# A reduction over three weight matrices on ScalarE: its loads alternated between two borrowed buffers, and more of them issued per step

## The reference

```python
q = _rmsnorm(x @ wq.T + bq, gq).reshape(B, L, H, D)     # B=4, L=2048, H=16, D=128
k = _rmsnorm(x @ wk.T + bk, gk).reshape(B, L, H, D)
v = (x @ wv.T + bv).reshape(B, L, H, D)
...                                                     # scores on 16 shifts, softmax, mix of v
x = _layernorm(x + out @ wo.T + bo)

def _quantize(w):
    gamma = jnp.mean(jnp.abs(w))
    return jnp.clip(jnp.round(w / (gamma + 1e-8)), -1.0, 1.0)
def _bitlinear(x, w):
    return jnp.matmul(x, _quantize(w).T)
hidden = sigmoid(_bitlinear(x, w1)) * _bitlinear(x, w2)  # w1, w2: 5632 x 2048
x = _layernorm(x + _bitlinear(hidden, w3))               # w3: 2048 x 5632
```

## Time and profile before

| | us |
|---|---|
| runs, lower and higher | 8750.89, 9032.59 |
| median of the two | 8891.74 |
| profiled execution | 8730.72 |
| its span on the slowest core (core 4) | 8729.2 |
| spans of the eight cores | 8706.3 to 8729.2 |

### The profile page before, as it was taken

One profiled execution on the slowest core, in us unless ns is written; L12 is line 12 of the kernel. 1 busy time (PEld: TensorE's weight loads), 2 busy tenths in 40 slices (PEclk: granted clock), 3 DMA queues, 4 the chain that ended last, 5 costly groups with the idle time before them and its releaser, 6 DMA issues. The chain is left out here.

```text
span 8729.2 us, 69946 instructions; the slowest of 8 cores (8706.3 to 8729.2 us)
## 1 busy us (share of the span) xinstructions
PE 5297.4 (61%) x24300; PEld 2462.2 (28%) x24680; DVE 3486.7 (40%) x4731; ACT 678.8 (8%) x737; POOL 811.0 (9%) x468
## 2 busy tenths in 40 slices
PE   6878878688883017771200001882789778878883
PEld 3443433344331001111100001441334333333331
DVE  4222222422221014336768887227542441442424
ACT  0012222100222210000000000000000000000000
POOL 0000000000000003550074400000000001001000
PEclk7889988788896558995555555885889889889896
DMA  2222222221223331005643333002212113114114
GB/s 94 73 90 74 83 85 73 102 71 68 94 74 110 125 109 51 29 21 139 167 145 129 131 130 125 29 20 96 75 51 75 58 41 119 53 46 123 49 53 158
DMA packets 254343, 750.12 MB, mean 86 GB/s; under 512 B 119596, under 2 KB 119852, under 8 KB 193324
## 3 DMA queue, kind: packets, MB, share of 16 engines
q1 hardware_dynamic: 80820, 418.42, 14.6%
q10 hardware_dynamic: 163576, 295.74, 10.0%
q0 software_dynamic: 9600, 31.47, 1.2%
HBM read 630.20 MB, written 115.34 MB: 85 GB/s over the span
## 5 line engine op out<-in xcount | busy, mean ns | idle before, releaser
L71 ACT ACT_TABLE_LOAD x223 | 286.1, 1283 | 7595.2 <-DVE tiny L71 2411.6
L71 DVE SCALAR_TENSOR_TENSOR accb<-vwV,attn,accb 128x128 f32<-128x128 f32 x1200 | 654.9, 546 | 169.4 <-DMA vwV<-v_h 75.4
L71 POOL TENSOR_TENSOR prodb<-qe,knorm 128x1024 f32<-128x1024 f32 (+14 forms) x184 | 320.0, 1739 | 3596.7 <-DVE knorm L71 3568.0
L1070 PE MATMUL pt4a<-c_id,accb 128*128 128x128 f32 x64 | 17.4, 427 | 982.2 <-DVE accb L71 974.4
L1332 PE MATMUL pb<-x2T_lo,qwt 128*128 128x512 bf16 x1408 | 574.5, 408 | 11.5 <-issue 9.1
L1386 PE MATMUL pb<-qw3s,stash_hi 128*128 128x512 bf16 x1352 | 525.0, 388 | 75.8 <-DMA qw3s<-qw3t_h 54.0
L1387 PE MATMUL pb<-qw3s,stash_lo 128*128 128x512 bf16 x1408 | 546.4, 388 | 3.5 <-issue 0.7
L1303 PE MATMUL pb<-x2T_lo,qwt 128*128 128x512 bf16 x1408 | 534.4, 380 | 2.5 <-issue 0.2
L1331 PE MATMUL pb<-x2T_hi,qwt 128*128 128x512 bf16 x1321 | 535.4, 405 | 0.0
L1302 PE MATMUL pb<-x2T_hi,qwt 128*128 128x512 bf16 x1363 | 517.3, 380 | 0.0
L71 POOL DMA_DIRECT2D qw3s<-qw3t_h x176 | 96.1, 546 | 3414.1 <-PE pb L1387 1763.7
(11 more groups left out here) (215 smaller groups left out, 9392.5 us busy)
## 6 DMA issues: line engine op xcount, KB each, us to landing
gbuf<-w ACTq DMA_DIRECT2D x88, 1024.0 KB, 6.3
fw<-w SPq DMA_DIRECT2D x88, 1024.0 KB, 4.9
vwV<-v_h SPq DMA_DIRECT2D x74, 1024.0 KB, 4.8
vwG<-v_h ACTq DMA_DIRECT2D x47, 1024.0 KB, 5.5
gbuf<-w ACTq DMA_DIRECT2D x64, 704.0 KB, 4.1
fw<-w SPq DMA_DIRECT2D x64, 704.0 KB, 4.1
wfb<-wv SPq DMA_DIRECT2D x32, 1024.0 KB, 5.0
wfb<-wk SPq DMA_DIRECT2D x32, 1024.0 KB, 6.0
```

Of the source, the lines that this page charges most:

```text
L71: return fn(*a, **k)
```

## The change

- The tile `gbuf0` is gone. Jobs load into `xbuf[k % 2]`, where k counts the jobs.
- `_gS_block` issues the load of job k first and then waits for the load of job k-1 and computes on it. One job stays pending (`gpendS`) from one call of `emit_gamma` to the next; a call with `drain=True` also computes the last pending one.
- Two waits on ScalarE are new for each job: for `x_tp` up to the value it has behind `p1` of this half, and, from job 2 on, for the `Abs` of job k-2, which used the same buffer.
- `emit_gamma(4)` stands behind each strip in place of 3, and `emit_gamma(2)` behind each block in place of 1. The first half now does 4x4 + 32x2 = 80 jobs, the second 4x4 + 16x2 = 48, the last call the remaining 24, all of 704 KB.
- Ahead of `rs_build("q")` there is a call that only drains.

```diff
-    gbuf = [xsc.sb("gbuf0", [128, 2048])]
...
     g_emit = [0]
-
-    def emit_gamma(n):
+    gcntS = [0]; gpendS = [None]
+    gxtp = [0]
+
+    def _gS_block(e, jobs, drain):
+        gab = S("g_ab")
+        for (src, col, w) in jobs:
+            k = gcntS[0]; gcntS[0] += 1
+            e.wait_ge(S("x_tp").h, gxtp[0])
+            if k >= 2:
+                e.wait_ge(gab.h, k - 1)
+            sm = ring_issue("gld", k)
+            sm.inc(e.dma_start(out=xbuf[k % 2][:, 0:w], in_=src), 16)
+            ring_rec("gld", k, sm)
+            if gpendS[0] is not None:
+                pk, pcol, pw = gpendS[0]
+                ring_wait(e, "gld", pk)
+                gab.inc(e.activation(xbuf[pk % 2][:, 0:pw], xbuf[pk % 2][:, 0:pw],
+                                     ACT.Abs, accum_out=gacc[:, pcol:pcol + 1]), 1)
+            gpendS[0] = (k, col, w)
+        if drain and gpendS[0] is not None:
+            pk, pcol, pw = gpendS[0]; gpendS[0] = None
+            ring_wait(e, "gld", pk)
+            gab.inc(e.activation(xbuf[pk % 2][:, 0:pw], xbuf[pk % 2][:, 0:pw],
+                                 ACT.Abs, accum_out=gacc[:, pcol:pcol + 1]), 1)
+
+    def emit_gamma(n, drain=False):
         j0 = g_emit[0]; j1 = min(j0 + n, len(gamma_jobs)); g_emit[0] = j1
-        if j1 <= j0:
-            return
-        gab = S("g_ab")
-        def fa(e):
-            for ji in range(j0, j1):
-                src, col, w = gamma_jobs[ji]
-                sm = ring_issue("gld", ji)
-                sm.inc(e.dma_start(out=gbuf[0][:, 0:w], in_=src), 16)
-                ring_rec("gld", ji, sm)
-                ring_wait(e, "gld", ji)
-                gab.inc(e.activation(gbuf[0][:, 0:w], gbuf[0][:, 0:w], ACT.Abs,
-                                     accum_out=gacc[:, col:col + 1]), 1)
-        on("scalar", fa)
+        sjobs = [gamma_jobs[j] for j in range(j0, j1)]
+        if sjobs or drain:
+            on("scalar", lambda e, sjobs=sjobs, drain=drain: _gS_block(e, sjobs, drain))
...
-            emit_gamma(3)
+            emit_gamma(4)
...
-            emit_gamma(1)
+            emit_gamma(2)
...
     p1(0)
+    gxtp[0] = S("x_tp").n
     p2v(0)
     p2kq("k", 0)
     p2kq("q", 0)
+    emit_gamma(0, drain=True)
     rs_build("q")
     barrier(recycle=False)
     p1(1)
+    gxtp[0] = S("x_tp").n
     p2v(1)
     p2kq("k", 1)
-    emit_gamma(1000)
+    emit_gamma(1000, drain=True)
```

More of the change, by code:

```diff
@@ L328, in build_nc, with _gjob @@
     gamma_jobs = []
[L329 to L332, removed]
+    def _gjob(src_, w_):
+        gamma_jobs.append((src_, len(gamma_jobs), w_))
+    for nm in ("w1", "w2"):
+        for gt in range(44):
+            _gjob(ins[nm][gt * 128:(gt + 1) * 128, :], 2048)
     for dt_ in range(16):
         for qt in range(4):
-            gamma_jobs.append((ins["w3"][dt_ * 128:(dt_ + 1) * 128, qt * 1408:(qt + 1) * 1408],
-                               88 + dt_ * 4 + qt, 1408))
+            _gjob(ins["w3"][dt_ * 128:(dt_ + 1) * 128, qt * 1408:(qt + 1) * 1408], 1408)
```

## The result

| | before | after |
|---|---|---|
| timed runs: median (lowest to highest), us | 8930.62 (8724.12 to 9275.65), 10 runs | 8456.79 (8314.93 to 8787.2), 11 runs |
| profiled execution, us | 8730.72 | 8331.64 |
| its span on the slowest core, us | 8729.2 | 8330.1 |
| median span of cores 0 to 3, of cores 4 to 7, us | 8715.8, 8722.8 | 8310.4, 8317.5 |

The changed kernel takes 0.9525 of the time before, 95% interval 0.9499 to 0.9551. The forecast was 8331 us, by the terms 0.953 of the profiled execution before (8320.6 / 8730.7).

A forecast was written before the change was run, and what follows sets the result against it. Bound: the core waiting on ScalarE's serial load and `Abs` turns before the square root. Profiled 8730.7 - 412.1 + 2.0 = 8320.6 us, plus half of 20 us for timed runs: 8331 us, range 8295 to 8465.

The forecast's parts named there:

- The bound: First stage, 2732 to 3208 us: the core waits on serial load and `Abs` turns; TensorE's wait for the square root is 494.9 us.
- The tail's length: The 24 jobs left after the last block: last `Abs` ends at 2795.6 instead of 3207.7 us, saving 412.1 us.
- a job's turn: Time per job after the last block: 2.89 us, as two jobs share 5.78; bounds 2.1 and 5.78 us.
- The weighing of the two loads: Whether two loads in flight overlap, 2.89 us a job, or serialize whole, 4.1 us a job with 383 us saved.
- The trace's side: Two 1 MB loads in flight landed in 6.1 and 8.1 us, one alone in 4.9: only the transfers queue up.
- The end of the first half: Last jobs and draining call before the first half's square root: +2.0 us, 0 if the load is quick, up to +5.
- What was costed at nothing: Extra jobs in blocks and at strip turns, weight loads beside them, new waits and TensorE's clock: all taken as 0 us.
- the covers: Time hiding the added work: 16.8 us ScalarE idle per block, 15.0 us per `wfb` load, next store at 255.96 us.
- Rival 2: At the 8 strip turns `wfb` lands late, giving back 16 to 75 us; time 8347 to 8406; chance 0.09.
- Rival 3: Jobs in the 48 blocks outgrow ScalarE's 16.8 us idle and become the path; 8906 us and more; chance 0.02.
- The level of the time: Placing the sum among timed runs: the lower run is 20 us above the profiled one, so half was added, giving 8331 us.

## Why the prediction was right or wrong

- **The bound.** Right. One wait of 494.9 us was the hole, and the time went from there: 405 us less at that wait, 405 us less in the median spans of both dies.
- **The tail's length.** Right in mechanism, short by 7 us. As the calls count, 26 loads of 704 KB went out from the last block on. From the issue of load 126 to the end of the last `Abs`, 79.8 us were worked out and 87.2 measured (2717.74 to 2804.89). The mis-sized term is a job's turn, 3.13 us for 2.89, 5.8 us over 24 jobs. Two things went into it. The sum took the landing of a load that is alone, 4.25 us to its use; with two in flight it took 4.45 at the end of the hole and longer before. And the gap from the end of an `Abs` to the next issue is 0.1 us now (2798.74 to 2798.85), where 0.06 stood before; two more waits stand in between now, but no run shows that they are the reason. The rest, 1.6 us, is in the first two jobs.
- **The weighing of the two loads.** The trace's side was right. The Trainium skill (SBUF — State Buffer, "Can I just issue two DMAs to hit both halves?") says of two concurrent DMAs, one on a tile at partition 0 and one on a tile at partition 64, that they gained 6% over one. Here a second load in flight took a job's turn from 5.78 to 3.13 us and a third to 2.47, near the 2.16 of ScalarE's own work, since of a landing of 4.1 us only about half is transfer (an estimate: the 2.1 to 2.2 us of the DMA engines that the prediction works out from the earlier trace rows). The traces agree with queueing only where the DMA engines are nearly full: with three in flight at a share of 0.88, the landing grew to 5.6 us.
- **The end of the first half.** +2.0 us worked out, +2.5 measured at the wait for `qsums` (11.5 to 14.0).
- **What was costed at nothing.** No cost is seen in any of it, as the covers were wide. The blocks keep their length with two, three and five jobs. But the work under the cover was put too low. From the first issue in a block to the end of its last `Abs` +10.3 us were worked out, and with 1 MB jobs it took 14.1 (642.72 to 656.82), since the block's first load was used 12.1 us after its issue (654.81), not 8.1; ScalarE kept 14.39 us of idle time there. At a strip's turn the jobs took 21.7 us (206.89 to 228.56), not 16 to 20, with the next store at 254.86. The share of the DMA engines at the turn went from 0.72 to 0.84 and the `wfb` loads took 10.7 us at most, and not even eight jobs made them late. (Rival 2's upper bound, 8 turns x 9 us, is 72 us and not 75.) The granted clock behind the hole is 0.89 (2823 to 3297 us) where it was 0.88.
- **Rival 3's price.** Its mechanism and order (squares, stores, `evb`) are those of the kernel with eight jobs, and so is its account: a block should grow by what its jobs last beyond 9.6 + 16.8 = 26.4 us. With eight they last 34.3 us (733.98 to 768.28), 7.9 beyond it, and this block is 7.9 us longer (39.4 in place of 31.5; 6.0 in the mean of all blocks). The two jobs of the change are far from that, and five of 1 MB cost the blocks nothing.
- **The level of the time.** This is the step that failed. The sum in the profiled execution's own time, 8320.6, was 11 us off (8331.64). That the forecast of 8331 us agrees with that execution is luck, as the 10 us added for the level of the timed runs made up for those 11. The text put the forecast by the lower of the two timed runs, by adding half of the 20 us between that run and the profiled execution, and let the range end at 8465, where "one of a pair falls that high again" lifts the median by 1.6%. The runs measured since show that the lowest run is not where the time lies: the median of ten runs before, 8930.62 us, is 2.4% above the lowest of them, and that of eleven runs after, 8456.79, is 1.7% above theirs and 126 us above the forecast. Set against the median that the prediction had in hand, 8891.74, the measured ratio makes 8469.4 us, just beyond the range's end, and the text's own ratio, 0.953, makes 8474. A forecast of a ratio had to be put on the median of the runs, and its range around that; the profiled execution's time is only the frame in which the terms add up. That the sum came within 11 us was no luck in its large term, the tail; its small misses (7 us there, 0.5 at the first half) went the same way.

## What to carry to other kernels

Where only half of a load's landing is transfer, a second buffer pays. Jobs whose results nobody needs until the end of a stage are worth more under another engine's work than overlapped behind it: here the counts alone brought 339 us, the buffers alone 231, and the buffers 66 on top of the counts. How many fit is read from the idle time of the engine that issues them, block by block, and it should be filled until nothing is left behind the stage; here it took three a block, where two were chosen. And a forecast made in one profiled execution gives a ratio: put it on the median of the runs, not on the lowest of them.

## What had not been expected of the hardware

With three loads in flight, core 0 moved 293 GB/s over 45 us at a DMA share of 0.88, and it was not alone: in the same stretch of their own spans cores 1, 2, 3, 6 and 7 moved 282 to 290 GB/s, while cores 4 and 5 were still in their k blocks, at 83 and 126. With two in flight all eight were in the hole and moved 224 to 245 each. So no run shows all eight with three loads in flight. What more loads in flight cost was landing time: 4.1 us for 704 KB with one, 4.3 with two, 5.6 with three.
